# An attention layer's output stage: transposed tiles against numerators scaled in place, eight consecutive tokens per partition

## Chip, core and metric

The kernel runs on one core of a Trainium2 chip, in one launch. Its time is the device time of that core in microseconds. 2926.12 us is the median of three runs before the change (2924.99 to 2928.0). Five engines work side by side, each through its own list of instructions, and meet only at semaphores: TensorE (PE: products, and PEld, its weight loads), VectorE (DVE), ScalarE (ACT), GpSimd (POOL) and SyncE (SP), which here issues nearly all DMAs.

## What is computed

One transformer block with modulation: attention over 16 batches of 1024 tokens with 256 features in 16 heads, then eight experts on rows chosen by index from the first two batches. Cut to what matters here:

```python
h = layernorm(x) * (1 + ca) + sa
xn = layernorm(h) * ln_gamma + ln_beta
q, k, v = heads(xn @ Wq + bq), heads(xn @ Wk + bk), heads(xn @ Wv + bv)   # q, k rotated
probs = softmax(causal(q k^T / 4))
o = (probs @ v) back to (B, L, D)
x = x + ga * (h + o @ Wo + bo)          # the output stage
h2 = layernorm(x) * (1 + cb) + sb       # then the experts, gathered by top_idx
```

`ga` is one row of 256 per batch, so `ga * (o @ Wo)` is `o @ (Wo * ga)`, and `ga * h` is the normalised `x` times a row (`a2`) plus a row that goes with the bias.

## The kernel before

Five stages, each a block with a barrier behind it. phase0 makes constants and the modulation rows. phase1 normalises `x`, projects and rotates it and stores queries, keys and values to HBM in bf16 parts; it also leaves the scale and shift of every row of `x` on chip (`rsx`, `nmx`, row p of tile t being token 128 t + p). phase2 is attention, in 64 units of one batch and four heads. For the unit two ahead TensorE fills PSUM banks with scores, in 19 slots of a unit (L1148, L1155), and VectorE takes their maxima (`largest`, L1069); for the present unit it forms scores again (L1173), ScalarE takes the exponential (L1113), GpSimd cuts the diagonal (L1008) and TensorE weighs the values (L1192). The values carry columns of ones, so that each head's 32 rows of the result are 16 numerators and 16 copies of the sum of the exponentials. `copy_out` (L1101) brings them out of PSUM in two halves, and SP stores them to `att` in HBM (L972).

phase3 is the output stage, batch after batch, in eight tiles of 128 tokens. Per tile TensorE turns four blocks of `att` so that tokens lie in partitions (L1516); VectorE inverts 16 sums (L1420) and multiplies (L1424); TensorE turns the result back (L1524), ScalarE copies it out of PSUM (L1470), and TensorE forms the bias (L1534) and the product with the weights that VectorE scaled by the gate (L1413, L1536). Beside this ScalarE normalises the tile of `x` (L1445), GpSimd multiplies it by `a2` and adds `x` (L1484, L1486, into `res`), and VectorE adds product and `res` (L1432). TensorE's order is written out: the transpositions of tile t, the second turn of tile t - 1, the product of tile t - 2. `res` has room for two batches. SP loads a batch two ahead and stores the finished one (`load`, `load_x`, `store`). In between, spread over batches 2 to 8, the chosen rows of the first two batches are normalised again (`prepare`, `choose`, `scale`): VectorE's statistics in batches 2 and 3, a root on ScalarE in batch 4, then sixteen steps of one instruction on each of three engines. The first experts' weights are loaded in batches 5 to 8, and GpSimd gathers their rows behind batches 12 and 13 (L1257). phase4 runs the experts.

## Time and profile before

| | us |
|---|---|
| median of the runs | 2926.12 |
| the profiled execution | 2926.05 |
| its span, first to last instruction | 2924.3 |
| attention in it (545 to 2338) | 1793 |
| output stage in it (2342 to 2626) | 284 |
| experts in it (2626 to 2916) | 290 |

The span is the time from the first to the last instruction in the trace. A stage is read from its stretch of the trace: how long each engine was busy there, what TensorE's granted clock was (1.00 is 2.4 GHz), and what share of the time the 16 DMA engines moved data. Busy TensorE is not TensorE at its peak, since its instructions overlap; the distance from the start of one to the start of the next tells more.

### The profile page before, as it was taken

The page shows a single profiled execution, that of the slowest core. Times are in us where ns is not written, and L with a number is a line of the kernel's source. Part 1 is how long each engine was busy: PE and PEld are TensorE (multiplying, and loading weights), DVE is VectorE, ACT ScalarE, POOL GpSimd, SP SyncE. Part 2 cuts the span into 40 slices and gives each one's busy share as a digit, 9 for nine tenths or more (in the row PEclk, how much of TensorE's full clock was granted, in tenths as well). Part 3 has the DMA queues.
Part 4 walks back from the last instruction along what each step waited for, and adds up shares of the span by engine and source line. Part 5 has one row for each costly group of instructions (what it writes and reads, how often), then busy time and mean ns, then how long its engine had stood idle before and what let it go on. Part 6 is the DMA issues. An engine that isn't in the chain of part 4 may idle for free. (4 is left out here: it accounts for less than half of the span.)

```text
span 2924.3 us, 48254 instructions
## 1 busy us (share of the span) xinstructions
PE 2748.3 (94%) x17467; PEld 1332.0 (46%) x17467; DVE 2083.7 (71%) x2857; ACT 1823.0 (62%) x3739; POOL 1026.3 (35%) x1554
## 2 busy tenths in 40 slices
PE   3999996999999999999999999999999879989997
PEld 1555552344444444444344443444444256766664
DVE  6999996877777777777777777777777246652221
ACT  2788882477777777777777777777777735432221
POOL 5899973121211212112121111212112158762331
PEclk6999996899999999999999999999999989999999
DMA  4688879345445354453544545444453088952432
GB/s 122 194 261 260 261 236 242 63 84 105 92 93 106 81 109 90 95 101 84 111 88 97 97 89 107 88 101 97 88 107 82 20 284 304 314 196 57 112 92 44
DMA packets 188321, 384.09 MB, mean 131 GB/s; under 512 B 33667, under 2 KB 105795, under 8 KB 175574
## 3 DMA queue, kind: packets, MB, share of 16 engines
q1 hardware_dynamic: 180038, 372.08, 49.9%
q0 software_dynamic: 6144, 8.52, 1.7%
q8 instruction: 141, 2.31, 0.4%
q14 instruction: 94, 0.77, 0.1%
q10 hardware_dynamic: 1904, 0.40, 0.1%
HBM read 238.55 MB, written 144.53 MB: 131 GB/s over the span
## 5 line engine op out<-in xcount | busy, mean ns | idle before, releaser
L1069 DVE TENSOR_REDUCE mx<-ps 128x2 f32<-128x1024 f32 (+3 forms) x1216 | 1371.0, 1166 | 408.6 <-PE ps L1155 313.2
L1113 ACT ACTIVATE prob<-ps 128x512 f32<-128x512 f32 (+1 forms) x2560 | 1251.8, 560 | 526.5 <-PE ps L1173 517.7
L1148 PE MATMUL ps<-k_rows,q_rows 96*128 96x512 bf16 (+3 forms) x3072 | 911.0, 332 | 32.4 <-PEq L420 25.7
L1173 PE MATMUL ps<-q_rows,k_rows 99*128 99x512 bf16 (+3 forms) x3072 | 907.1, 328 | 14.7 <-ACT prob L1113 6.1
L1008 POOL TENSOR_SCALAR_AFFINE_SELECT prob<-prob 128x512 f32<-128x512 f32 x512 | 319.9, 637 | 1451.3 <-ACT prob L1113 1451.3
L1192 PE MATMUL ps<-prob,v_rows 128*32 128x512 f32 (+3 forms) x6144 | 628.3, 496 | 0.0
L1173 PEld LDWEIGHTS ps<-q_rows,k_rows 99*128 99x128 bf16 x3072 | 273.1, 98 | 599.1 <-ACT prob L1113 360.3
L1148 PEld LDWEIGHTS ps<-k_rows,q_rows 96*128 96x128 bf16 x3072 | 290.1, 98 | 262.6 <-DVE mx L1069 60.7
L1155 PE MATMUL ps<-mask_b,unit_b 128*128 128x128 bf16 (+2 forms) x1408 | 348.5, 248 | 0.0
L1192 PEld LDWEIGHTS ps<-prob,v_rows 128*32 128x32 f32 x6144 | 134.3, 108 | 245.8 <-ACT prob L1113 122.9
L792 PE MATMUL ps<-x_t,w_all 128*128 128x512 f32 x512 | 231.6, 595 | 0.0
L1686 DVE SCALAR_TENSOR_TENSOR y<-ps,gx,gate 128x256 f32<-128x256 f32 x32 | 15.5, 484 | 196.4 <-PE ps L1775 196.4
L1155 PEld LDWEIGHTS ps<-mask_b,unit_b 128*128 128x128 bf16 x1408 | 139.4, 99 | 22.9
L1536 PE MATMUL ps<-wg,n_t 128*128 128x256 f32 x512 | 145.7, 407 | 0.0
L747 POOL TENSOR_TENSOR stage<-rest,stage 128x1024 bf16<-128x1024 f32 x64 | 136.7, 2136 | 24.5 <-ACT stage L677 24.5
L1470 ACT COPY n_t<-ps 128x256 f32<-128x256 f32 x128 | 47.5, 371 | 148.6 <-PE ps L1524 148.4
L792 PEld LDWEIGHTS ps<-x_t,w_all 128*128 128x128 f32 x512 | 94.2, 191 | 93.5 <-issue 92.7
L800 PE MATMUL ps<-w_all,x_t 128*128 128x256 f32 x512 | 124.6, 386 | 2.1
L1611 POOL DMA_INDIRECT sum_rows<-ys,dest x32 | 50.1, 1565 | 213.0 <-ACT ys L1698 154.7
L1775 PE MATMUL ps<-w,hid 128*128 128x256 f32 x512 | 119.1, 386 | 0.0
L1484 POOL TENSOR_TENSOR res_b<-res_b,a_b 128x256 f32<-128x256 f32 x128 | 96.3, 753 | 59.1 <-ACT res_b L1445 58.8
L1761 PE MATMUL ps<-gx_t,w 128*128 128x512 f32 x256 | 114.7, 601 | 1.3 <-ACT hid L1706 0.4
(174 smaller groups left out, 2606.4 us busy)
## 6 DMA issues: line engine op xcount, KB each, us to landing
k_rows<-k_parts SPq DMA_DIRECT2D x384, 128.0 KB, 7.3
v_ones<-v_st SPq DMA_DIRECT2D x64, 512.0 KB, 6.5
v_rows<-v_ones SPq DMA_DIRECT2D x64, 512.0 KB, 9.3
att<-o_sb SPq DMA_DIRECT2D x128, 256.0 KB, 2.3
att_b<-att SPq DMA_DIRECT2D x16, 2048.0 KB, 9.9
q_rows<-q_parts SPq DMA_DIRECT2D x64, 384.0 KB, 4.6
q_parts<-stage SPq DMA_DIRECT2D x120, 192.0 KB, 3.3
k_parts<-stage SPq DMA_DIRECT2D x120, 192.0 KB, 3.4
```

Source lines behind the costliest of these rows:

```text
L747: pool.tensor_tensor(parts(n, 2), rest[:, n % 2], parts(n, 1), ALU.subtract).then_inc(lo_done, 1)
L792: ins = pe.matmul(half(n, e), w_all[:, k, c * P:(c + 1) * P], x_t[:, blk, k, :], start=(k == 0), stop=(k == KC - 1))
L800: ins = pe.matmul(o, x_t[:, t // 4, k, t % 4 * P:t % 4 * P + P], w_all[:, k, 2 * D:3 * D], start=(k == 0), stop=(k == KC - 1))
L1008: pool.affine_select(out=own, in_=own, compare_op=ALU.is_ge, fill=0.0, base=0, pattern=[[0, HG], [1, P]], channel_multiplier=-1).then_inc( ...
L1069: dve.tensor_reduce(dst, src, AX.X, ALU.max).then_inc(a_free, 1)
L1113: nc.scalar.activation(prob[:, (g * NPC + i) % RING, h, 0:w], src, ACT.Exp).then_inc(exp_done, 1)
L1148: ins = pe.matmul(ps[:, at, col:col + w], q[g][0:ROWS, h, i * P:(i + 1) * P], k[g][0:ROWS, h, k0:k0 + w], start=(r == 0), stop=True, skip_ ...
L1155: ins = pe.matmul(own, unit_b[:, :], mask_b[:, :].rearrange("p (o n) -> p o n", o=1) .to_broadcast([P, per, P]), start=False, stop=True, s ...
L1173: ins = pe.matmul(ps[:, PS_B + bank(g, n), at:at + w], k[g][0:AUG, h, j * P:(j + 1) * P], q[g][0:AUG, h, q0:q0 + w], start=True, stop=True)
L1192: ins = pe.matmul(ps[32 * h:32 * h + 32, PS_O, col:col + w], v[g][:, j, h, :], prob[:, (g * NPC + i) % RING, h, at:at + w], start=(j == 0) ...
L1536: ins = pe.matmul(o, n_t[:, r % 2, k, :], wg[:, p, k, :], start=False, stop=(k == KC - 1))
L1775: ins = pe.matmul(o, hid[:, f, c * P:(c + 1) * P], w2[:, e % 2, f, :], start=False, stop=(f == FT - 1))
```

## The change

The output stage no longer turns anything. `att` is read as it lies, features in partitions, and only its numerators. The inverses of the sums are made during attention, one batch behind: SP loads a batch's 16 rows of sums into 128 partitions (`load_sums`), VectorE inverts them and splits the result into three bf16 parts (`invert_sums`), SP stores them (`save_inverse`) and later loads them as 48 rows (`load_inverse`). In the output stage TensorE multiplies them with a matrix of ones and zeros (`rows`), which spreads each head's inverse over its 16 features (`spread_rec`, four products of 512 columns per batch), and VectorE multiplies numerators by that (`normalise`, 512 elements each) into `n_t`, from which the product is formed straight away. The four of the next batch stand among the tiles of the present one.

A tile now is every eighth token: partition p holds tokens 8 p to 8 p + 7, so that rows of `x` and of the result are 8 KB of consecutive bytes per partition. `normalise` writes with a step for that, and the scales and shifts of the rows, which phase1 leaves in the other order, go through HBM: SP stores them per batch during attention (`row_stats`) and loads them in the new order. In the last batch of attention SP also loads what the first two or three batches of the output stage need. The product has four PSUM banks in place of two, `x` a ring of three in place of four. In phase0 two pairs of semaphores become one each.

```diff
+def load_sums(sp, o, att_d, b):
+    reuse(sp, o.inv_step, INV_STEPS * b)
+    sums = att_d[b].rearrange("g (h n) t -> (g h) n t", n=2 * (P // HG // 2))[:, P // HG // 2, :]
+    sp.dma_start(o.den[:, :], sums.rearrange("h (a c) -> h a c", c=P)).then_inc(o.den_in, DMA)
...
+def invert_sums(dve, o, b):
+    done = lambda n: INV_STEPS * b + n
+    dve.wait_ge(o.den_in, (b + 1) * DMA)
+    reuse(dve, o.inv_stored, b * DMA)
+    dve.reciprocal(o.inv[:, :], o.den[:, :]).then_inc(o.inv_step, 1)
+    dve.wait_ge(o.inv_step, done(1))
+    dve.tensor_copy(o.inv3[:, 0, :], o.inv[:, :]).then_inc(o.inv_step, 1)
...
+def load_numerators(sp, o, att_d, b):
+    KC = o.num.shape[2]
+    for k in range(KC):
+        mine = att_d[b, k * NG // KC:(k + 1) * NG // KC].rearrange("g (h n) t -> (g h) n t", n=2 * (P // HG // 2))
+        sp.dma_start(o.num[:, b % 2, k, :], mine[:, 0:P // HG // 2, :]).then_inc(o.num_in[b % 2], DMA)
...
                 store(un, 0)
+                output_rows(b, g)
+
+            def output_rows(b, g):
+                if g == 0 and b >= 2:
+                    save_inverse(sp, o, rec_d, b - 2)
+                if g == 1:
+                    with nc.allow_non_contiguous_dma("statistics go to the order of tokens"):
+                        sp.dma_start(stat_d[0, b].rearrange("(t p) -> p t", p=P), rsx[:, b, :]).then_inc(o.stat_stored, DMA)
+                        sp.dma_start(stat_d[1, b].rearrange("(t p) -> p t", p=P), nmx[:, b, :]).then_inc(o.stat_stored, DMA)
...
+                if g == 2 and b >= 1:
+                    for c in range(2):
+                        sp.wait_ge(o_stored[c], b * NG * DMA)
+                    load_sums(sp, o, att_d, b - 1)
+                if g == 2 and b == LAST:
+                    sp.wait_ge(o.stat_stored, 2 * B * DMA)
...
+                    for n in range(2):
+                        load_gate(sp, o, mods_d, out_bias_d, n)
+                        load_numerators(sp, o, att_d, n)
+                        load_inverse(sp, o, rec_d, n)
+                        load_residual(sp, o, x, mods_d, n)
...
+                if g == NG - 1 and b >= 1:
+                    invert_sums(dve, o, b - 1)
...
+            load_sums(sp, o, att_d, B - 1)
             for b in range(B):
+                if b + 2 < B:
+                    load_small(b + 2)
+                    load_num(b + 2)
                 if b + XR - 1 < B and b >= 1:
-                    load_x(sp, b + XR - 1)
+                    load_x(b + XR - 1)
+                if b == 1:
+                    save_inverse(sp, o, rec_d, B - 1)
+                if b + 3 < B:
+                    load_rec(b + 3)
...
+                store(b)
...
+            def normalise(b, q):
+                k, half = q % KC, q // KC
+                at = slice(half * HALF, (half + 1) * HALF)
...
+                dve.wait_ge(spread, b * NQ + q + 1)
+                tiles = lambda v: v.rearrange("d (p t) -> d p t", t=T)
+                dst = n_t[:, b % 2, k, :].rearrange("d (t p) -> d p t", t=T)[:, half * P // 2:(half + 1) * P // 2, :]
+                dve.tensor_tensor(dst, tiles(num[:, b % 2, k, at]), tiles(ps[:, PS_R + q % 2, :]), ALU.mult) \
+                   .then_inc(norm_done, 1)
...
+            for b in range(B):
+                if b + 1 < B:
+                    scale_weights(b + 1)
+                for t in range(T):
+                    if t == 1 and b == 0:
+                        invert_sums(dve, o, B - 1)
+                    finish(b, t)
+                    prepare((b - SB) * T + t)
+                    if t in NORM_AT and b + 1 < B:
+                        normalise(b + 1, NORM_AT.index(t))
...
-                reuse(act, x2_done, b * T - T)
+                reuse(act, x2_done, (b - 2) * T + t + 1)
...
+            for b in range(B):
+                for t in range(T):
+                    product(b, t)
+                    if t in SPREAD_AT and b + 1 < B:
+                        spread_rec(b + 1, SPREAD_AT.index(t))
```

GpSimd's two operations per tile, and its place in the stage, are as they were.

TensorE in the output stage, from the stage's first products on, before the change (`att_b` the transpositions, `norm` the second turn, `ob_b` the bias, `wg` the product):

```order
L1516 MATMUL ps<-ident,att_b 128x128 x8
L1524 MATMUL ps<-ident,norm 128x128 x2
L1516 MATMUL ps<-ident,att_b 128x128 x4
L1524 MATMUL ps<-ident,norm 128x128 x2
L1534 MATMUL ps<-ob_b,ones 128x256
L1536 MATMUL ps<-wg,n_t 128x256 x2
L1516 MATMUL ps<-ident,att_b 128x128 x4
L1524 MATMUL ps<-ident,norm 128x128 x2
L1534 MATMUL ps<-ob_b,ones 128x256
L1536 MATMUL ps<-wg,n_t 128x256 x2
```

The same place in the changed kernel (`head_rows` is the matrix that spreads):

```order
L1641 MATMUL ps<-rec,head_rows 128x512 x4
L1651 MATMUL ps<-ob_b,ones 128x256
L1653 MATMUL ps<-wg,n_t 128x256 x2
L1641 MATMUL ps<-rec,head_rows 128x512
L1651 MATMUL ps<-ob_b,ones 128x256
L1653 MATMUL ps<-wg,n_t 128x256 x2
L1641 MATMUL ps<-rec,head_rows 128x512
L1651 MATMUL ps<-ob_b,ones 128x256
L1653 MATMUL ps<-wg,n_t 128x256 x2
L1651 MATMUL ps<-ob_b,ones 128x256
```

Six transpositions per tile are gone, and four products of 512 columns per batch have come.

VectorE in attention where one unit's maxima end and the next one's begin, behind the last heads of a batch, in the changed kernel (`den` the sums, `inv` their inverse and its parts; before the change the maxima follow one another directly there):

```order
L1190 TENSOR_REDUCE mx<-ps 128x2 x4
L900 RECIPROCAL inv<-den 128x128
L902 CAST inv<-inv 128x128
L904 TENSOR_TENSOR inv_rest<-inv 128x128
L906 CAST inv<-inv_rest 128x128
L908 TENSOR_TENSOR inv<-inv_rest,inv 128x128
L1190 TENSOR_REDUCE mx<-ps 128x2x4
L1190 TENSOR_REDUCE mx<-ps 128x4
```

Five operations of VectorE, with a wait for the load of `den` ahead of them, stand in front of the next unit's first maxima.

SP from the last batch's third unit to the end of attention in the changed kernel, where four stores of `att` stood in a row before:

```order
L1061 DMA att<-o_sb 128x512
L887 DMA den<-att 128x1x128
L1103 DMA rs_wide<-row_stats 128x16x8
L1103 DMA nm_wide<-row_stats 128x16x8
L931 DMA gate_b<-mods 128x256
L932 DMA ob_b<-out_bias_parts 3x256
L920 DMA num<-att 128x1x1024 x2
L913 DMA rec<-rec_sums 48x1024
L926 DMA x_b<-in_L_attn_x 128x2048
L927 DMA a_b<-mods 128x256
```

Behind these come the same loads for the second batch, the rows of a third and its inverses, and only then the last three stores.

## Rows read from the trace of the kernel before

**Rows 1.** Stretches: length, each engine's busy time (instructions), clock, DMA share, GB/s.

```profile
545.00:2338.00 1793.00, 1778.29 (x13562) 727.40 (x13564) 1358.46 (x1360) 1306.70 (x2675) 357.83 (x634) 1.00 0.44 92
2342.00:2626.00 284.00, 254.46 (x1408) 191.32 (x1408) 167.56 (x467) 119.25 (x274) 205.32 (x281) 0.97 0.83 278
```

**Rows 2.** TensorE in order of time, one tile: start, duration, engine, line, operation, operands.

```profile
2444.88 1.13 PE L1536 MATMUL ps<-wg,n_t 128*128 128x256 f32 x4
2445.84 0.60 PE L1516 MATMUL ps<-ident,att_b 128*128 128x128 f32 x4
...
2446.60 0.28 PE L1534 MATMUL ps<-ob_b,ones 3*128 3x256 bf16 x1
2446.80 1.13 PE L1536 MATMUL ps<-wg,n_t 128*128 128x256 f32 x4
```

**Rows 3.** Groups in 2342 to 2626: busy us, mean ns, idle before.

```profile
L1484 POOL TENSOR_TENSOR res_b<-res_b,a_b 128x256 f32<-128x256 f32 x128 | 96.3, 753 | 59.1 <-ACT res_b L1445 58.8
L1486 POOL TENSOR_TENSOR res_b<-res_b,x_b 128x256 f32<-128x256 f32 x128 | 93.5, 731 | 10.0
...
L1424 DVE TENSOR_TENSOR norm<-ps,rec 128x256 f32<-128x256 f32 x128 | 54.3, 424 | 4.6 <-DVE rec L1420 0.2
...
L1432 DVE TENSOR_TENSOR x<-ps,res_b 128x256 f32<-128x256 f32 x112 | 47.5, 424 | 80.0 <-PE ps L1536 77.4 <-POOL res_b L1486 1.6 <-issue 1.1
...
L1420 DVE RECIPROCAL rec<-ps 128x16 f32<-128x16 f32 x128 | 32.1, 251 | 11.5 <-PE ps L1516 10.5
...
L1413 DVE TENSOR_TENSOR wg<-wo,gate_b 128x256 f32<-128x256 f32 x32 | 15.4, 523 | 56.6 <-DMA ob_b<-out_bias_parts 56.6
...
L1257 POOL DMA_INDIRECT gx<-tok_rows,idx x8 | 7.9, 985 | 2.1 <-issue 2.0
...
L1393 DVE BATCH_NORM_STATS2 st<-x_all 128x6 f32<-128x256 f32 x16 | 6.7, 418 | 0.0
```

**Rows 4.** GpSimd in order of time, two tiles near the stage's start.

```profile
2357.04 0.73 POOL L1484 TENSOR_TENSOR res_b<-res_b,a_b 128x256 f32<-128x256 f32 x1
...
2358.53 0.73 POOL L1484 TENSOR_TENSOR res_b<-res_b,a_b 128x256 f32<-128x256 f32 x1
```

**Rows 5.** In order of time: the stage's first transfer, TensorE's first work, last sum.

```profile
2341.70 0.32 SPq L1325 DMA_DIRECT2D gate_b<-mods  x1
...
2350.77 1.97 PE L1516 MATMUL ps<-ident,att_b 128*128 128x128 f32 x8 [12.22 <-DMA att_b<-att]
...
2624.91 0.42 DVE L1432 TENSOR_TENSOR x<-ps,res_b 128x256 f32<-128x256 f32 x1 [0.84 <-PE ps L1536]
```

**Rows 6.** TensorE in order of time, the stage's first product.

```profile
2357.15 2.08 PE L1536 MATMUL ps<-wg,n_t 128*128 128x256 f32 x4
```

**Rows 7.** Attention at a unit's end in order of time: VectorE's maxima, TensorE's fill.

```profile
1408.86 2.36 DVE L1069 TENSOR_REDUCE mx<-ps 128x2 f32<-128x1024 f32 x2 [0.92 <-PE ps L1155]
1412.06 2.36 DVE L1069 TENSOR_REDUCE mx<-ps 128x8 f32<-128x1024 f32 x2 [0.84 <-PE ps L1155]
...
1415.17 0.33 PE L1148 MATMUL ps<-k_rows,q_rows 96*128 96x384 bf16 x1
```

**Rows 8.** VectorE in order of time, in the set-up: a reciprocal, a cast.

```profile
7.90 1.74 DVE L339 RECIPROCAL e<-e 16x256 f32<-16x256 f32 x1
...
39.73 0.23 DVE L626 CAST unit_b<-ident 128x128 bf16<-128x128 f32 x1 [1.84 <-PEq L147]
```

**Rows 9.** SP in order of time: the last batch's third unit is stored.

```profile
2310.95 0.34 SPq L972 DMA_DIRECT2D att<-o_sb  x1
```

**Rows 10.** DMA issues by line: count, size of each, median us to landing.

```profile
tok_rows<-in_L_ffn_combine_weights SPq DMA_DIRECT2D x1, 64.0 KB, 4.6
ident<-in_const_ident SPq DMA_DIRECT2D x1, 64.0 KB, 2.0
```

**Rows 11.** Stretches as in rows 1: the end of attention, a busy batch.

```profile
2290.00:2300.00 10.00, 8.20 (x57) 2.21 (x57) 0.00 (x0) 8.47 (x20) 1.61 (x3) 1.00 0.08 29
2440.00:2457.00 17.00, 15.38 (x88) 11.71 (x88) 11.91 (x31) 8.81 (x20) 14.06 (x20) 1.00 0.95 325
```

307 lines of the change are left out of this document (167 added, 140 removed).

## Prediction

> **What bounds the kernel now.** I read the stages first [rows 1]: attention keeps TensorE busy for 1778 of 1793 us at full clock, and the output stage, which the change rewrites, takes 284 us with TensorE busy for 254, GpSimd for 205 and VectorE for 168. Then the order of one tile on TensorE in the middle of that stage [rows 2]: the product starts at 2444.88, the transpositions of later tiles follow at 2445.84, the bias at 2446.60, the next product at 2446.80. That is 1.92 us per tile without a gap: 0.96 product, 0.76 transpositions, 0.20 bias. Eight tiles are a batch, so TensorE alone needs 15.4 us of the roughly 17 that a batch takes (a sixteenth of the stage below, less its start), and it is the bound. Third, who comes next if TensorE gets less: the groups of that stage [rows 3]. GpSimd does two operations per tile, 753 + 731 = 1484 ns on average; VectorE's are shorter. When nothing holds it back GpSimd starts one tile every 1.49 us, from 2357.04 to 2358.53 [rows 4], so some 12 us per batch. Last the ends of the stage [rows 5]: its first transfer is issued at 2341.70, TensorE begins at 2350.77 after a wait for that data, and the last sum ends at 2624.91 + 0.42 = 2625.33. The stage is 283.6 us long.
>
> The sum goes against the profiled execution, 2926.05 us with a span of 2924.3; the median of the runs shown, 2926.12, is the same within 0.1 us. A difference of 0.2%, about 6 us, is what a measurement of this kernel can tell from none.
>
> **The output stage, TensorE.** The 48 transpositions of a batch go (8 x 0.76 = 6.1 us). Added are four products of 512 columns that spread the inverses; the trace has none here, and the nearest row is the bias, also bf16, 256 columns in 0.20 us [rows 2]. Between 0.2 (if the length cost nothing) and 0.42 each, I take 0.42: 1.7 us. A batch then costs 8 x 1.16 + 1.7 = 11.0 us.
>
> **VectorE.** Eight reciprocals and eight normalisations (251 and 424 ns) go. Four normalisations of 512 elements come, reading PSUM and writing with a step; the row is 424 ns for 256 [rows 3], so 0.42 to 0.85, and up to 1.3 if the step hurts. I take 0.7. With eight sums at 424 and two weight scalings at 523 ns a batch is 2.8 + 3.4 + 1.05 = 7.3 us. Batches 2 and 3 also carry eight statistics of 418 ns each and their small followers, some 12 us in all.
>
> **ScalarE** loses its copies out of PSUM and keeps the row normalisations; it was never late on its own account.
>
> **GpSimd loses nothing**, and so it becomes the bound. Its work is 128 tiles. An operation of 0.73 and its like-sized partner share a pitch of 1.49 [rows 4], so 0.03 us per tile lies between operations; with the averages of [rows 3], which hold the collisions with VectorE's scalings, a tile costs 1.484 + 0.03 = 1.51, together 194 us. Added are 16 multiplications for the chosen rows at about 0.75 (12 us) and the eight gathers (7.9 us and the 2.1 idle ahead of them, 10 us). It starts about 1 us into the stage, since rows, shifts and statistics were loaded during attention, and the last sum takes 0.4. That is 217.2 us against 283.6.
>
> **One stall remains.** In batch 4 ScalarE takes a root for which VectorE must have finished batches 2 and 3. TensorE starts cold: the first products show 2.08 us [rows 6] where the warm row shows 1.13 [rows 2]. Thus VectorE ends batch 3 some 55 us into the stage (5 for the start, about 14, 11, 12.5 and 12.5 for the batches), while GpSimd ends it at 1 + 4 x 12.1 = 49; ScalarE, blocked at the root, feeds it nothing more. I take 5 us, between 0 and 10. Stage: 222.2, so **61.4 us less**.
>
> **Transfers.** A batch now moves 1 MB of numerators (2 MB before), 1 MB of rows in, 1 MB out and 0.35 MB of small things, 3.5 million bytes; in 12.1 us this is 290 GB/s. A busy batch before moved 325 GB/s at a share of 0.95 [rows 11], so they stay just hidden, with a batch of lead. The experts' weights, 1 MB more in batches 5 to 8, fall where GpSimd has 2.9 us more per batch. Over the stage some 58 million bytes; at the stage's own mean of 278 GB/s [rows 1] that is 209 us, below 222.
>
> **Attention.** VectorE gets five operations per batch, between two units. The reciprocal of 128 elements lies between 0.25 us for 16 [rows 3] and 1.74 for 256 [rows 8], linearly 0.95; the four others, 128 elements each, at 0.23 like the cast in [rows 8]. With small gaps 2.0 us (1.6 to 2.8). What hides them: VectorE's last maximum of a unit ends at 1408.86 + 2.36 = 1411.22 and the next starts at 1412.06, 0.84 idle; the second one of that pair ends at 1414.42, and TensorE overwrites its banks at 1415.17, 0.75 later [rows 7]. Less 0.1 for the signal this is a cover of 1.5 us, and 0.5 remains, in which TensorE, the bound there, waits with everything queued behind. Fourteen such places (batch 14's falls where no maxima are left): **7 us more**, between 0 and 18.
>
> SP issues four DMAs more per batch. The two that write the statistics consist of 1024 pieces of 4 bytes each; the nearest row is 64 KB in pieces of 32 bytes, landed after 4.6 us [rows 10]; 2 to 10 us each. Queued behind them are the loads for three units ahead and the maxima of the next unit but one; half a unit, some 14 us, covers them, so I price them at zero. The Trainium skill speaks against them: its page "DMA: Bandwidth & Descriptors" says (Rules for kernel authors) that a non-contiguous last dimension becomes one descriptor per element, and (Specifications) that transfers under 512 B are read, changed and written back. By that they come out dear, and the sum would grow by what exceeds the cover; by the row of 4.6 us it does not change. No run here shows a 4-byte write yet.
>
> At the end of attention SP issues some 6.2 million bytes of first rows and 4096 pieces of statistics behind the store at 2310.95 [rows 9]: 19 us at 325 GB/s plus up to 9, until about 2340; two late stores stand behind them, and the stage began at 2341.70 [rows 5]. **1.5 us more** (0 to 6). In the set-up a wait for the small input now also takes the identity, which lands 2.0 us after its issue [rows 10]: **0.5 us more** (0 to 2).
>
> **Sum:** 2926.05 - 61.4 + 7 + 1.5 + 0.5 = 2873.7, say 2874 us.
>
> **Rivals.** (a) Something else bounds the stage: transfers, or VectorE if the stepped write takes 1.3 us. Transfers decide when the rate falls under 58 / 222 = 261 GB/s; at 240 the stage is 242 us and the time 2893. For it: a batch of lead only and loads that blocked SP before; against it: 325 GB/s in [rows 11]. (b) Nothing of the inversions is hidden: 14 x 2.0 = 28 instead of 7, 2895. For it: TensorE has no gaps in attention; against it: the 0.84 and 0.75 us of [rows 7]. (c) Neither the stall nor the inversions nor the end of attention cost anything: 2926 - 66 = 2860. (d) **Slower than before:** TensorE's clock. GpSimd-bound, TensorE idles for 0.3 us in each 1.5. If the clock then stayed at 1.2 GHz, everything doubles as between [rows 6] and [rows 2], a batch costs 22 us, the stage 352, and the time is about 3003. It decides when the mean batch exceeds 17.1 us, that is when over half of the stage runs slow. Against it stands the end of attention, where TensorE was busy for 8.20 of 10 us, waiting many times for ScalarE, with a granted clock of 1.00 [rows 11]. The Trainium skill has such a case: "TensorE: Matmul & The Clock Gate" (A second HAM failure mode) tells of a kernel whose short pauses between groups of products let the clock swing between its levels; the trace here does not agree, with the 1.00 just named. (e) The 4-byte stores block the queue: slower only if each batch pays over 3.3 us beyond the cover.
>
> **How the numbers follow.** Forecast 0.58, (a) 0.15, (b) 0.10, (c) 0.10, (d) 0.03, (e) 0.02; 0.02 for no change, if TensorE and VectorE keep each other at the old pace. The forecast's own bounds are 2860 to 2890; with (a), (b) and (c) the range is 2858 to 2898. Faster 0.93, same 0.02, slower 0.05.
>
> **What would show it.** Right: the stage some 222 us long, GpSimd busy for about 95% of it, its pitch near 1.5 us, TensorE waiting for VectorE's sums, clock at 1.00 after the start; in attention a gap of about half a microsecond on TensorE behind each batch's reciprocal. Wrong: GpSimd waiting for ScalarE or for rows throughout, TensorE waiting for numerators, a granted clock under 0.9 in mid-stage, or an attention longer by over 20 us.

## The result

The changed kernel takes 2984.61 us (median of 4 runs, 2977.94 to 2990.92) against 2925.97 before (the median of the three runs named above and a fourth): a ratio of 1.020, 95% interval 1.018 to 1.022. It is slower by 59 us where 52 us less were forecast. The profiled execution took 2987.96 us, its span 2986.1, so 61.8 us more than the span before.

The stretches of the changed kernel, attention and output stage (length, busy time and instructions of TensorE, its weight loads, VectorE, ScalarE and GpSimd, granted clock, DMA share, GB/s), stand against [rows 1]:

```profile
545.00:2440.00 1895.00, 1817.55 (x13539) 733.64 (x13537) 1385.12 (x1434) 1310.14 (x2671) 356.20 (x632) 0.97 0.46 91
2445.00:2690.00 245.00, 219.55 (x704) 119.94 (x704) 149.73 (x280) 74.54 (x146) 206.32 (x281) 0.82 0.75 238
```

Attention has grown by some 100 us, and its clock is no longer 1.00. The output stage is shorter, but its clock is 0.82 (before 0.97) and its transfers run at 238 GB/s (before 278). Its ends, in order of time, against [rows 5]:

```profile
2444.87 0.54 SPq L887 DMA_DIRECT2D den<-att  x1
...
2687.14 0.42 DVE L1534 TENSOR_TENSOR x<-ps,res_b 128x256 f32<-128x256 f32 x1 [0.85 <-PE ps L1653]
```

It lasts from 2444.87 to 2687.56, 242.7 us: 40.9 less than before, where 61.4 less were forecast. It begins 103.2 us later than before. Attention proper, from SP's first load of maxima to the output stage's first transfer, takes 1922.3 us in place of 1817.6, so 104.7 more; the set-up in front of it is 1.6 us shorter, the experts behind the stage 0.4.

**The standstills.** Waits by engine, the line that waited and what ended the wait (us in total, times, longest), in attention of the changed kernel:

```profile
ACT prob L1241 <- remote: 57.4, 14, 6.4
DVE mx L1190 <- remote: 52.7, 14, 5.4
...
PEld ps L1276 <- DVE mx L1190: 45.8, 143, 2.5
```

"remote" means that the profile has no event on this core which would explain the end of the wait. There was no such wait before the change. In 15 of the 16 batches such waits end 12 to 19 us after the batch's two stores of `row_stats` were issued; only behind the sixth batch's there is none. One of them, first SP (the two stores of `row_stats`), then ScalarE, VectorE and TensorE, each row with its start and duration:

```profile
2247.54 0.43 SPq L1089 DMA_DIRECT2D row_stats<-rsx  x1
2248.01 1.69 SPq L1090 DMA_DIRECT2D row_stats<-nmx  x1
...
2261.35 2.06 ACT L1241 ACTIVATE prob<-ps 128x512 f32<-128x512 f32 x4 [4.08 <-remote]
...
2261.45 0.96 DVE L1190 TENSOR_REDUCE mx<-ps 128x2 f32<-128x768 f32 x1 [3.11 <-remote]
...
2262.00 0.61 PE L1301 MATMUL ps<-q_rows,k_rows 99*128 99x384 bf16 x2 [2.60 <-ACT prob L1241]
```

The same place in steps of two microseconds, columns as in the stretches above:

```profile
2249.00:2251.00 2.00, 2.00 (x20) 1.24 (x22) 1.27 (x3) 1.72 (x4) 0.03 (x1) 1.00 0.47 16
2251.00:2253.00 2.00, 2.00 (x18) 0.88 (x11) 1.08 (x2) 1.29 (x4) 1.22 (x2) 1.00 0.36 0
2253.00:2255.00 2.00, 2.00 (x18) 0.69 (x16) 2.00 (x2) 0.78 (x3) 0.63 (x1) 1.00 0.00 0
...
2259.00:2261.00 2.00, 0.40 (x4) 0.12 (x2) 0.00 (x0) 0.00 (x0) 0.00 (x0) 1.00 0.00 0
2261.00:2263.00 2.00, 1.00 (x8) 0.43 (x10) 0.96 (x1) 1.65 (x4) 0.00 (x0) 0.59 0.00 0
2263.00:2265.00 2.00, 2.00 (x14) 0.90 (x14) 1.30 (x3) 1.30 (x4) 1.22 (x2) 0.50 0.00 0
```

The small pieces occupy the DMA engines until about 2253 and move next to nothing (the share is 0.36 at 0 GB/s). Some six microseconds later all four engines stand still at once, and ScalarE and VectorE go on within 0.1 us of each other. TensorE then works at half clock (0.50) for a while. A batch thus loses the standstill, and TensorE's work behind it at the lower clock comes on top; how the loss divides between the two is not measured.

**The end of attention.** ScalarE, and SP, whose three last stores of `att` are folded into one row with the time from the first to the last:

```profile
2441.65 0.58 ACT L1229 COPY o_sb<-ps 128x512 f32<-128x512 f32 x1 [11.13 <-DMA att<-o_sb]
```

```profile
2422.53 20.09 SPq L1061 DMA_DIRECT2D att<-o_sb  x3
```

The last copy out of PSUM waited 11.13 us for a store that stood behind the preloads.

**In the output stage**, groups of instructions (busy us, mean ns, idle before and what ended it), against [rows 3]:

```profile
L1609 POOL TENSOR_TENSOR res_b<-res_b,a_b 128x256 f32<-128x256 f32 x128 | 97.5, 762 | 22.0 <-ACT res_b L1579 21.7 <-issue 0.3
L1611 POOL TENSOR_TENSOR res_b<-res_b,x_b 128x256 f32<-128x256 f32 x128 | 94.3, 736 | 10.0
L1579 ACT ACTIVATE res_b<-x_b,nm_wide,rs_wide 128x256 f32<-128x256 f32 x128 | 66.6, 588 | 142.7 <-DMA a_b<-mods 131.1 <-DVE x_all L1534 9.0 <-PEq L987 2.7
L1524 DVE TENSOR_TENSOR n_t<-num,ps 128x512 f32<-128x512 f32 x64 | 66.1, 1039 | 19.5 <-DMA num<-att 16.9 <-PE ps L1653 2.4
...
L1511 DVE TENSOR_TENSOR wg<-wo,gate_b 128x256 f32<-128x256 f32 x32 | 23.3, 768 | 39.3 <-PEq L987 34.9 <-DMA ob_b<-out_bias_parts 4.4
```

GpSimd's operations are nearly as long as before (762 and 736 ns, 753 and 731 before), and it is busy for 206 of 243 us, that is 85%, not 95%. ScalarE, which feeds it, waited 131 us for rows. The normalisation takes 1.04 us, not 0.7.

### The profile page after: what moved, and what is told of

Read it like the earlier page. It is cut to its first block and busy times, and to the rows that moved or that the text cites. A ratio compares the mean times of both kernels' runs of the same rounds, so it can differ in the third digit from the quotient of the medians.

```text
span 2986.1 us, 46292 instructions
## 1 busy us (share of the span) xinstructions
PE 2753.6 (92%) x16763; PEld 1268.2 (42%) x16763; DVE 2092.3 (70%) x2746; ACT 1783.4 (60%) x3611; POOL 1022.4 (34%) x1554
## 2 busy tenths in 40 slices
DMA packets 202793, 371.66 MB, mean 124 GB/s; under 512 B 78099, under 2 KB 119507, under 8 KB 185958
## 5 line engine op out<-in xcount | busy, mean ns | idle before, releaser
L1301 PE MATMUL ps<-q_rows,k_rows 99*128 99x512 bf16 (+3 forms) x3072 | 920.3, 333 | 59.1 <-ACT prob L1241 48.8
L1320 PE MATMUL ps<-prob,v_rows 128*32 128x512 f32 (+3 forms) x6144 | 641.9, 506 | 0.0
L1653 PE MATMUL ps<-wg,n_t 128*128 128x256 f32 x512 | 173.0, 468 | 0.0
L1579 ACT ACTIVATE res_b<-x_b,nm_wide,rs_wide 128x256 f32<-128x256 f32 x128 | 66.6, 588 | 142.7 <-DMA a_b<-mods 131.1
L1653 PEld LDWEIGHTS ps<-wg,n_t 128*128 128x128 f32 x512 | 102.1, 221 | 29.2 <-issue 6.9
```

The costliest lines, as they stand in the source:

```text
L1301: ins = pe.matmul(ps[:, PS_B + bank(g, n), at:at + w], k[g][0:AUG, h, j * P:(j + 1) * P], q[g][0:AUG, h, q0:q0 + w], start=True, stop=True)
L1320: ins = pe.matmul(ps[32 * h:32 * h + 32, PS_O, col:col + w], v[g][:, j, h, :], prob[:, (g * NPC + i) % RING, h, at:at + w], start=(j == 0) ...
L1653: ins = pe.matmul(c, n_t[:, b % 2, k, t * P:(t + 1) * P], wg[:, b % 2, k, :], start=False, stop=(k == KC - 1))
```

## The experiments

All times stand against the kernel before, measured on the same chip in the same series (medians 2925.97 to 2928.06). The sections up to the inversions are about attention. Lengths of a stage come from the one profiled execution of each kernel; the runs of one kernel of the later sections lie up to 22 us apart, so a few microseconds between two such stages tell little.

### Is it the 4-byte stores? The change without them

```diff
-                if g == 1:
-                    ... sp.dma_start(stat_d[0, b].rearrange("(t p) -> p t", p=P), rsx[:, b, :])
-                    ... sp.dma_start(stat_d[1, b].rearrange("(t p) -> p t", p=P), nmx[:, b, :])
+                if g == 1 and b == 0:
+                    sp.wait_ge(o.stat_copied, 1)
+                    sp.dma_start(stat_d.rearrange("n b (t p) -> (b t) n p", p=P), o.stat[:, :, :])
...
+                for n, src in enumerate((rsx, nmx)):          # TensorE, ahead of attention
+                    ins = pe.transpose(ps[:, PS_O, n * P:(n + 1) * P], src..., ident[:, :])
```

> The changed kernel, with one thing different: the 32 stores of row_stats in pieces of 4 bytes are gone. TensorE turns rsx and nmx once, ahead of attention (two transpositions into the bank of the results), ScalarE copies them out, and SP stores them with one DMA of 256 pieces of 512 bytes. Theory A (the 4-byte stores make all engines stand still for 2 to 6 us, 11 to 15 us after their issue, and cool TensorE's clock): the waits named remote vanish, the output stage begins near 2354 instead of 2445, the time falls by about 90 us to 2890 to 2900, below the kernel before. Theory B (the inversions or the DMAs that belong to them cause the standstills, 15 of them too): the output stage still begins near 2440 and the time stays near 2980. Theory C (the time in attention goes into both): in between, and the rest then shows at the inversions on VectorE.

Measured: 2898.95 us (4 runs), ratio 0.990, interval 0.988 to 0.992. The output stage begins at 2355.03, and no wait is named remote. So 85.7 us of the changed kernel's time hang on these 32 stores, 5.4 per batch, and without them the change is a gain. Theory A.

### The stores alone, on the kernel before

```diff
                 store(un, 0)
+                if g == 1:
+                    for n, src in enumerate((rsx, nmx)):
+                        sp.dma_start(stat_d[n, b].rearrange("(t p) -> p t", p=P), src[:, b, :])
```

> The kernel before, and nothing of the change in it but the 32 stores of row_stats in pieces of 4 bytes (two per batch, behind the store of the second unit's first half), which nobody reads. Theory A (these stores alone stop the engines): one standstill per batch 11 to 15 us behind them, attention longer by 80 to 95 us, the time 3005 to 3020. Theory B (the inversions cause it): within 10 us of 2926.

Measured: 3036.12 us in one run, 110 more than before: 6.9 us per batch. One standstill, in steps of two microseconds (the stores were issued at 940.59 and 941.07):

```profile
950.00:952.00 2.00, 1.58 (x20) 0.89 (x12) 0.52 (x2) 0.00 (x0) 0.20 (x1) 1.00 0.00 0
952.00:954.00 2.00, 0.00 (x0) 0.00 (x0) 0.00 (x0) 0.00 (x0) 0.00 (x0) 1.00 0.00 0
954.00:956.00 2.00, 0.00 (x0) 0.00 (x0) 0.00 (x0) 0.00 (x0) 0.00 (x0) 0.80 0.00 0
956.00:958.00 2.00, 0.83 (x4) 0.39 (x4) 0.96 (x1) 1.09 (x2) 0.00 (x0) 0.50 0.00 0
```

ScalarE and VectorE, as they go on:

```profile
956.51 1.09 ACT L1120 ACTIVATE prob<-ps 128x512 f32<-128x512 f32 x2 [7.07 <-remote]
956.66 0.96 DVE L1076 TENSOR_REDUCE mx<-ps 128x2 f32<-128x768 f32 x1 [6.14 <-remote]
```

TensorE's last products before this ended near 951.6, and both engines wait here only for semaphores that TensorE's products raise, so what they waited for was done 5 us earlier. The stores stop the engines with nothing else of the change present. The loss was even larger than expected (3005 to 3020).

### The same bytes in pieces of 32 bytes

```diff
-sp.dma_start(stat_d[n, b].rearrange("(t p) -> p t", p=P), src[:, b, :])
+sp.dma_start(stat_d[n, b].rearrange("(p t) -> p t", p=P), src[:, b, :])
```

> The kernel before with the same 32 stores of the same bytes at the same places, but in pieces of 32 bytes (each partition's eight values stay together; nobody reads them). If the number of pieces decides (128 instead of 1024 per store): no standstill, within 5 us of 2926. If two more stores per batch on SP's queue decide, whatever their pieces: as with the 4-byte stores, 3005 to 3020. If an HBM write below 512 bytes decides by itself: standstills shorter in the ratio of the pieces, 0.6 us each, 2935.

Measured: 2926.49 us, one run: no cost, no standstill. Two more stores per batch on SP's queue are harmless by themselves.

### 4-byte loads in place of stores

```diff
-sp.dma_start(stat_d[n, b].rearrange("(t p) -> p t", p=P), src[:, b, :])
+sp.dma_start(spare[:, n, b, :], x_flat[b, n * L:(n + 1) * L].rearrange("(t p) -> p t", p=P))
```

> The kernel before with 32 loads in pieces of 4 bytes (1024 pieces each, 4 KB of x into a spare tile, at the places where the stores of row_stats would be; nobody uses them). If 4-byte pieces stop the engines in either direction, by their number: standstills and 3010 to 3036, as with the stores. If only small writes to HBM do: no standstill, within 5 us of 2926; a few us more at most from queueing on SP.

Measured: 2927.55 us, one run: no cost. The number of pieces and their size do not do it in the direction of reading.

### Half as many stores

```diff
-for n, src in enumerate((rsx, nmx)):
+for n, src in enumerate((rsx,)):
```

> The kernel before with only one of the two 4-byte stores per batch (rsx, 1024 pieces; nobody reads them). Both together cost 110 us, 6.9 per batch. If the standstill is proportional to the pieces: 2975 to 2985. If a fixed time per batch or per event: 3020 to 3036. If only what exceeds some room that hides the first pieces counts: 2930 to 2960.

Measured: 2930.4 us, one run, 4 more than before, and inside the range of the kernel before in the same series (2923.46 to 2931.13); attention is 2.6 us longer, and no wait is named remote. Half the pieces do not cost half. There is room in which they cost nearly nothing, and beyond it the cost is steep.

### 4-byte stores 512 bytes and 64 bytes apart

```diff
-stat_d = nc.dram_tensor("row_stats", [2, B, L], F32, ...)
+stat_d = nc.dram_tensor("row_stats", [2, B, L, P], F32, ...)     # second kernel: 16 in place of P
...
+sp.dma_start(stat_d[n, b, :, 0].rearrange("(t p) -> p t", p=P), src[:, b, :])
```

> The kernel before with both 4-byte stores per batch, each piece 512 bytes from the next one in HBM (the receiving tensor has 128 places per value, one is written; nobody reads them). If the standstill comes from neighbouring pieces falling into the same line of memory from several DMA engines at once: gone or small, 2926 to 2945. If every small write costs by itself: as when they lie side by side, 3010 to 3040.

> The kernel before with both 4-byte stores per batch, each piece 64 bytes from the next one (512 bytes apart they cost nothing, side by side 110 us; nobody reads them). If the pieces disturb each other only within 64 bytes: 2922 to 2930. If the unit in which they collide is larger, up to 512 bytes: in the ratio of neighbours, 8 instead of 128 in 512 bytes, 2930 to 2945, or as side by side, 3036.

Measured: 2923.75 us with 512 bytes between them, 2928.67 with 64, one run each: no cost in either. The same 32768 small writes are free when they lie 64 bytes apart. So it is not the small write by itself that costs, but many small writes beside each other.

### The two stores half a batch apart

```diff
-                if g == 1: rsx and nmx
+                if g in (1, 3): rsx at 1, nmx at 3
```

> The kernel before with both 4-byte stores per batch side by side in HBM, but half a batch apart: rsx behind the second unit's first half, nmx behind the fourth's. One store alone per batch cost 4 us in all, both together 110. If the time that the standstill takes grows once the pieces outstanding together exceed what is hidden: 2930 to 2936, twice the 4 us. If the number of pieces per batch decides, or nmx's place in memory: 3010 to 3036.

Measured: 2933.05 us, one run: 7 more than before in place of 110, and of that only 1.0 us in attention (1818.6 us in place of 1817.6). As many neighbouring small writes, but fewer of them at once, stop nothing.

### The same in the changed kernel

```diff
                     sp.dma_start(stat_d[0, b]..., rsx[:, b, :])
-                    sp.dma_start(stat_d[1, b]..., nmx[:, b, :])
+                if g == (3 if b < LAST else 0):
+                    sp.dma_start(stat_d[1, b]..., nmx[:, b, :])
```

> The changed kernel with one line moved: nmx is stored half a batch after rsx (behind the fourth unit's first half, in the last batch behind the first's), still in pieces of 4 bytes side by side. Theory A (what stops the engines is the number of neighbouring small writes under way at once; on the kernel before this spacing took the cost from 110 to 7 us): no long standstills, the output stage begins near 2357, 2899 to 2910, much as with the turned statistics. Rival (in the changed kernel the further DMAs of the inversions lie close enough to bring the standstill back): 2940 to 2985.

Measured: 2904.2 us (2 runs), ratio 0.992, interval 0.990 to 0.995. The output stage begins at 2353.55. No wait is named remote. One moved line turns the loss of 59 us into a gain of 22.

### The inversions alone

```diff
+                if g == 0 and b >= 2:
+                    save_inverse(sp, o, rec_d, b - 2)
+                if g == 2 and b >= 1:
+                    for c in range(2):
+                        sp.wait_ge(o_stored[c], b * NG * DMA)
+                    load_sums(sp, o, att_d, b - 1)
...
+                if g == NG - 1 and b >= 1:
+                    invert_sums(dve, o, b - 1)
```

> The kernel before with only the inversions added in attention: SP loads a batch's sums, VectorE inverts and splits them between two units, SP stores the three parts, which nobody reads; the output stage is as before. By the prediction's term (0.5 us uncovered at each of 14 places): plus 7 us, 2933, with a range of 0 to 18. By its rival (nothing is hidden): plus 28, 2954. If the inversions were what stops the engines: 3005 to 3020.

Measured: 2932.2 us (9 runs), ratio 1.0021, interval 1.0011 to 1.0031, so 3 to 9 us more; attention itself grows by 6.7. VectorE's groups in it:

```profile
L878 DVE RECIPROCAL inv<-den 128x128 f32<-128x128 f32 x15 | 14.1, 943 | 25.8 <-DMA den<-att 25.8
L886 DVE TENSOR_TENSOR inv<-inv_rest,inv 128x128 bf16<-128x128 f32 x15 | 4.9, 324 | 0.5
```

With the other three (292, 227 and 226 ns) a batch's five operations take 2.0 us. The one wait of 25.8 us lies at attention's end, where VectorE has no maxima left. What VectorE waited for TensorE's scores, and TensorE's weight loads for VectorE's maxima, before and with the inversions:

```profile
DVE mx L1069 <- PE ps L1155: 286.0, 370, 0.9
PEld ps L1148 <- DVE mx L1069: 32.2, 123, 0.3
```

```profile
DVE mx L1121 <- PE ps L1210: 264.7, 341, 0.9
PEld ps L1203 <- DVE mx L1121: 41.0, 151, 0.4
```

Of the 30 us of new work some 21 went into VectorE's own idle time, and TensorE waited 8.8 us more. The forecast's 7 us stands, and most of the work is hidden, as it said; the cover of 1.5 us per place was not measured by itself.

### The end of attention: late stores ahead of the preloads

From here on each kernel is held against the one with turned statistics (2899). All but the old order of tokens, which needs no statistics in HBM, contain its repair.

```diff
-                    for n in range(2): gate, numerators, inverses, rows     # all behind the third unit
-                    load_residual(sp, o, x, mods_d, 2)
+                    first_rows(0)                                           # behind the third unit
+                if g == 3 and b == LAST:
+                    first_rows(1)                                           # no rows of x
...
             def epilogue():
                 store(unit(LAST, NG - 1), 1)
+                load_residual(..., 1); load_residual(..., 2)
```

> The kernel with turned statistics (2899), and the preloads at the end of attention spread out: behind the third unit of the last batch only what batch 0 needs, behind the first store of the last unit the small things and numerators of batch 1, and the rows of batches 1 and 2 behind the very last store of att. Theory A (the late store waits behind 6 MB of preloads: ScalarE waits 8.9 us for it, and the block's end waits for SP, whose three late issues hold 18 us): the output stage begins 8 to 10 us earlier, near 2345; rows of batches 1 and 2 come later, at most 3 us given back; 2890 to 2893. Rival (what was moved is only paid later, in the stage, which is bound by transfers): within 3 us of 2899.

Measured: 2888.63 us (4 runs), ratio 0.987, interval 0.984 to 0.990; the stage begins at 2350.42 and lasts 243.5 us. ScalarE's last copy out of PSUM waits 1.87 us in place of 8.88. Of the 8.9 us between the two spans 4.1 are attention's and 4.3 the stage's (247.8 without this edit). That is near Theory A's time (2890 to 2893), but the stage begins 4.6 us earlier and not 8 to 10. The medians lie 10 us apart and the four runs of each kernel 12 and 17 us, so the size of the gain is uncertain. This kernel has the lowest median of the study among those that compute everything; four later ones (2889.3 to 2897.05) lie within its range of 2883.08 to 2899.8. It is faster than both given kernels.

### The old order of tokens

```diff
-x[b].rearrange("(p t) d -> p t d", p=P)
+x[b].rearrange("(t p) d -> p t d", p=P)
...
-                dve.tensor_tensor(dst, tiles(num...), tiles(ps...), ALU.mult)      # dst with a step
+                dve.tensor_tensor(n_t[:, b % 2, k, at], num[:, b % 2, k, at], ps[:, PS_R + q % 2, :], ALU.mult)
```

> The changed kernel with the old order of tokens: a tile is 128 consecutive tokens again, the rows of x and of the result move in pieces of 1 KB, the multiplication by the inverses writes without a step, and rsx and nmx are used as phase1 leaves them, so that no statistics go through HBM at all (no 4-byte stores, no loads of 32-byte pieces). Inverses, numerators, preloads, rings and orders stay as in the change. Theory A1 (the new order of tokens gains nothing but the stepped write costs): the multiplication falls from 1.04 to about 0.6 us, the time lies 5 to 15 us below the 2899 of the kernel with turned statistics, 2885 to 2894. Theory A2 (pieces of 8 KB are what makes transfers fast): the stage gets longer by about 10 us, 2905 to 2912. Theory A3 (neither matters, the order in which SP issues the loads bounds the stage): 2895 to 2902.

Measured: 2909.52 us (4 runs), ratio 0.994, interval 0.993 to 0.996, and a stage of 255.3 us. The multiplication falls to 677 ns as expected, and still the stage is 7.5 us longer than with turned statistics: as Theory A2 had it, pieces of 8 KB are worth more than the step costs. That VectorE's shorter work brought nothing also speaks against VectorE as the bound of the stage.

### TensorE kept warm at the start, and the root later

```diff
+            for n in range(8):                       # behind the last product of attention
+                keep_warm(pe, ps[:, 1, :], ident)
...
                 spread_rec(0, q)
+                for n in range((0, 2, 1, 2)[q]):
+                    keep_warm(pe, ps[:, 6, :], ident)
...
-    FIRST_H = NT + 6                                 # second kernel only
+    ROOT = NT + 10
+    FIRST_H = ROOT + 4
```

> The kernel with turned statistics and late stores first (2889), and thirteen products of TensorE whose result nobody reads: eight behind the last product of attention, where it waits about 7 us for the end of the stage, and five between the four that spread the first batch's inverses, where it waits for VectorE. Theory A (TensorE starts the stage at half clock because it stood still, and batch 0 takes 24 us instead of 13): the granted clock stays at 1.00 through the start, batch 0 ends some 10 us earlier, 2876 to 2882. Rival 1 (GpSimd's 208 us bound the stage anyway; the lost start is caught up): within 3 us of 2889. Rival 2 (the clock falls all the same at the waits for VectorE): within 3 us of 2889, the clock at 0.50 until 2376.

> As the next kernel (later rows behind the late stores, TensorE kept warm), and ScalarE's root for the chosen rows with all that hangs on it one batch later (eight tiles). Theory A (the root blocks ScalarE, because VectorE has not finished batches 2 and 3; 7.9 us at it, and GpSimd starves for some 20 us around 2385 to 2430): a further 5 to 10 us less than the next kernel, 2866 to 2876, with GpSimd busy for over 9 of 10 us from 2360 on. Rival (VectorE and the transfers are what is late there, the root only shows it): within 2 us of the next kernel.

Measured: 2894.64 us (0.988, 0.987 to 0.990) warm, 2889.3 (0.987, 0.985 to 0.988) warm and with the later root, against 2888.63 for the kernel both are built on: no gain that can be told (the runs of the three overlap). Ten microseconds behind the stage's start, without the warm products:

```profile
2360.00:2370.00 10.00, 10.00 (x22) 4.97 (x22) 6.35 (x10) 2.40 (x4) 9.53 (x14) 0.50 0.30 75
```

and with them:

```profile
2360.00:2370.00 10.00, 8.99 (x36) 4.98 (x34) 8.73 (x15) 3.67 (x7) 9.45 (x14) 1.00 0.30 90
```

The clock is 1.00 in place of 0.50 and TensorE does 36 instead of 22 products, yet the stage is 243.5 us long in both. What the start gains is waited for later: the cold start costs nothing as long as something else is late. Rival 1 of that expectation said this, but named GpSimd as the bound, which the last experiment does not bear out for this kernel; and 2894.64 lies outside its 3 us. With the later root the stage was 249.8 us long, in the slowest of that kernel's four runs (2899.72); the gain of 5 to 10 us that was expected of it did not come.

### Deeper rings, all repairs together, and gates early

```diff
-                    load_num(b + 2)                  # two buffers, waits for the fifth tile
-                    load_x(b + 2)                    # three buffers, queued behind it
+                    load_x(b + 3)                    # four buffers
+                    load_num(b + 3)                  # three buffers
...
-                    load_small(b + 2)                # third kernel only: gates in a ring of four
+                    load_small(b + 3)
```

> The kernel with turned statistics (2899), and deeper rings in the output stage: three buffers of numerators in place of two, four of rows in place of three (the added ones lie where queries and keys of the first unit lay), and SP issues both for the batch three ahead at the head of a batch, where nothing that they wait for is still open; the kernel before it issued numerators of two ahead behind the fifth tile, and rows behind these. Theory A (late issue makes ScalarE wait 133 us for rows and VectorE 21 us for numerators, and TensorE's clock falls in these waits): waits fall below 30 us, the stage from 248 to 222 to 230 us, 2873 to 2882. Rival (the transfers' rate is the bound, 58 MB at 270 GB/s): the waits stay, the stage is 240 or more, 2890 to 2899.

> All four repairs at once: turned statistics, late stores ahead of preloads, deeper rings with loads three batches ahead, TensorE kept warm and the root one batch later. If each was held back by the others (rings by the root, which grew to 25 us there; the warm start by rows that are late): 2868 to 2880. If the transfers' rate bounds the stage whatever the order: 2885 to 2895, as each alone.

> All four repairs together, and the gates' rows (which the weights are scaled by) in a ring of four, loaded three batches ahead like the rest; with all repairs but this one VectorE waited 51 us for the gate and the bias, which queue behind megabytes of rows and numerators issued before them. Theory A (small loads that land late are what took the gain of the deeper rings): that wait vanishes, the stage falls from 255 to 226 to 235 us, 2870 to 2882. Theory B (what moves in the stage, at the rate that the 16 engines reach, bounds it, and each order only shifts who waits): the wait moves to rows, numerators or inverses, 2885 to 2900.

Measured: 2897.05 us (0.990, 0.988 to 0.991) with rings alone, 2900.45 (0.989, 0.986 to 0.992) with all four repairs, 2891.23 (0.989, 0.987 to 0.991) with the gates too. The stage lasts 251.2, 255.5 and 239.1 us. With rings alone ScalarE's waits for rows fell from 133 to 66 us, but VectorE now waited 46 us for the gate's row, and ScalarE 25 at the root. All four repairs together came out above both expectations; their runs spread from 2882.39 to 2904.52, and the profile is of the slowest. There VectorE waits for the gate and the bias, and ScalarE still 65 us for rows:

```profile
DVE wg L1542 <- DMA ob_b<-out_bias_parts: 51.3, 12, 7.3
```

With the gates early VectorE's wait is gone, and these are the longest (with those for the fourth buffer of rows, 25.7, ScalarE's come to 85):

```profile
ACT res_b L1610 <- DMA a_b<-mods: 59.6, 7, 11.5
DVE x L1566 <- DMA out<-x: 40.8, 11, 9.8
```

Whatever is issued first, something else is late: first the rows, then the gates, then the stores of finished results, whose buffers are not free. This is what Theory B of the last expectation said, and 2891.23 lies in its range.

### Fewer transfers

```diff
-                if b + XR - 1 < B and b >= 1:
-                    load_x(b + XR - 1)
...
```

> The kernel with turned statistics and late stores first (2889), with the rows of x loaded for the first three batches only; what is left out: batches 3 to 15 add the rows of an earlier batch instead of their own, so that 14.8 MB of some 58 fewer are moved in the output stage. Theory A (the rate of the transfers, some 265 to 280 GB/s, bounds the stage): the stage falls from 245 to about 212, GpSimd's 208 us and its start, the time to 2855 to 2865. Theory B (the order of SP's issues, the cold start or the root bound it): within 8 us of 2889.

The kernel leaves out the rows of `x` of batches 3 to 15 and adds those of an earlier batch in their place, so its result is not the block's. By the trace's totals it moves 15.3 MB less (371.66 and 356.31), not 14.8.

Measured: 2875.57 us (2 runs), ratio 0.983, interval 0.981 to 0.985, against 2888.63 for the kernel it is built on. The stage lasts 225.7 us in place of 243.5. Its longest waits now are

```profile
ACT res_b L1588 <- DVE x L1543: 79.0, 68, 6.2
DVE x L1543 <- POOL res_b L1620: 45.5, 39, 5.6
```

ScalarE waits for room, VectorE for GpSimd, which is busy for 206 of 226 us: only now is GpSimd the bound, as the prediction had it for the changed kernel. So 13 us (between the medians) to 18 (between the profiled stages) hang on these loads. That is less than the 24 to 34 of Theory A and more than the 8 of Theory B. The edit also takes 26 DMAs out of SP's queue, so it does not part the rate of the transfers from their order.

## Why the prediction was wrong

**The step that failed first: the stores of `row_stats`, priced at zero.** The prediction saw 1024 pieces of 4 bytes, took 2 to 10 us each from [rows 10] and covered them with the half unit of SP's queue behind them. It priced the wrong resource. The loads behind the stores were hardly late (in attention keys landed 7.7 us after their issue on the median, 7.2 before the change; maxima 9.5, 9.1 before). Instead all engines stood still, the last of it 12 to 19 us after the issue, and TensorE's clock fell to 0.50 in both standstills shown. 85.7 us hang on it in the changed kernel, 110 on the kernel before. Rival (e) put the point at 3.3 us per batch and got 5.4, but as a blocked queue and with a chance of 0.02; it had no row for a 4-byte write and should have kept a wide end in the range. The rule of the Trainium skill that was weighed there ("DMA: Bandwidth & Descriptors", Rules for kernel authors and Specifications: one descriptor per element, writes under 512 B read, changed and written back) spoke in the right direction. The runs agree only in part: the same small writes 64 bytes apart cost nothing, so neither the descriptors nor the single small write are the price.

**The output stage, forecast 222.2, measured 242.7.** The step that failed is "they stay just hidden". The mean of 278 GB/s in [rows 1] was taken for what the stage can move at any time, and 58 million bytes came out as 209 us. But it moves little at its ends. The kernel before, its first 30 us:

```profile
2345.00:2375.00 30.00, 21.10 (x104) 16.05 (x104) 11.38 (x33) 8.82 (x21) 15.63 (x22) 0.74 0.91 308
```

The kernel with late stores first, its first 30 us, its middle and its last 30:

```profile
2345.00:2375.00 30.00, 22.56 (x59) 10.80 (x52) 16.03 (x24) 12.66 (x24) 22.88 (x33) 0.60 0.47 140
2375.00:2570.00 195.00, 174.09 (x597) 96.66 (x595) 125.37 (x238) 58.60 (x115) 165.69 (x225) 0.90 0.86 278
2570.00:2600.00 30.00, 21.82 (x68) 12.40 (x69) 11.00 (x27) 4.05 (x8) 17.45 (x25) 0.77 0.25 101
```

Where transfers ran at 308 GB/s at the start of the stage, they now run at 140, because SP waits there to store batch 0 before it may load more: it issues nothing from 2356.70 to 2376.39. In the changed kernel SP issues nothing from 2451.23 to 2465.97, when the store of batch 0 goes out, and its first 24 us are

```profile
2445.00:2457.00 12.00, 9.61 (x20) 4.37 (x21) 10.35 (x16) 9.00 (x18) 11.01 (x16) 0.50 0.36 99
2457.00:2469.00 12.00, 12.00 (x43) 6.54 (x42) 7.61 (x15) 3.60 (x6) 11.37 (x17) 0.90 0.24 91
```

The middle then has to carry the rest. With 15.3 MB fewer the stage takes 225.7 us, within 3.5 of the forecast, and there GpSimd is the bound. In the changed kernel itself it is not, so the mechanism of the forecast failed along with the number: the term of the transfers was zero in place of 13 to 18, measured on the kernel with late stores first. Rival (a) named transfers, with a stage of 242 us at 240 GB/s; the trace has 242.7 us and 238 GB/s. That these agree proves nothing more, since the mean rate is the same 58 million bytes over the length of the stage, whatever makes it long; what speaks for (a) are ScalarE's 131 us of waiting for rows and the kernel with fewer of them. Three signs of being wrong that the prediction named were there: ScalarE waiting for rows, a clock under 0.9, and attention longer by over 20 us.

**Smaller terms.** The inversions: 7 us forecast, 5.9 measured, right. The end of attention: 1.5 forecast; the wait was 11.13 us, and spreading the preloads brought back some 10 between the medians, about half of it in the stage. The step behind it took the last transfer at 2340 and the stage's old begin for a cover, and forgot that a copy out of PSUM waits for the store behind the preloads, and that the block's end waits for SP; it also counted two late stores where three stood behind the preloads. The set-up: 0.5 forecast, it got 1.6 shorter. The root's stall: 5 forecast; ScalarE waited 9.8 for it, and moving it gained nothing that can be told. The normalisation: 0.7 taken, 1.04 measured, inside its bounds of 0.42 to 1.3 and without effect, since VectorE is busy for 150 of 243 us.

**Rival (d), the clock.** The rows of the changed stage show it swing between its levels (0.50 and 1.00, 0.82 on the mean), so what the prediction quoted against it, 1.00 at the end of attention in [rows 11], did not carry over. The Trainium skill's case of a clock that swings with short pauses ("TensorE: Matmul & The Clock Gate", A second HAM failure mode) thus agrees with the trace as far as the swinging goes. At the start it was not what cost time: with 1.00 in place of 0.50 there, the stage was as long. For the middle no run tells. There are stretches such as this one of the changed kernel, in which TensorE is busy throughout at 0.50 and GpSimd for 3.38 of 12 us:

```profile
2505.00:2517.00 12.00, 12.00 (x26) 6.33 (x26) 5.63 (x16) 3.56 (x6) 3.38 (x6) 0.50 0.69 220
```

SP's loads stand behind stores of sums that wait for TensorE's products, so a slow TensorE can make rows late, and late rows can slow TensorE; which came first is not shown, and a part of the 20 us over the forecast may be the clock's. The stage as a whole was not doubled, as (d) had it.

Added up against the profiled execution: attention takes 1832.2 us in the kernel with turned statistics and 1922.3 in the changed one, so 90.2 for the stores; 6.7 for the inversions, measured alone; what is left of the 104.7, 7.9, for the end of attention. With 40.9 less in the stage and 2.0 less at both ends of the program this gives 61.8, the difference of the spans. It closes by construction, since the 7.9 is a remainder. The stage was 5.1 us longer with turned statistics than in the changed kernel, so the 85.7 between the medians is net of that.

**What stays open.** Why neighbouring small writes stop engines that have nothing to do with them is not shown: the trace tells only that ScalarE and VectorE got a signal some 5 us after the work it stands for. Nor is it shown whether the stage is held by the rate of the 16 engines, by the order in which their queue is served, or in part by TensorE's clock. Against the rate alone speaks that their share in the middle was 0.83 to 0.89 in every variant that loads all rows, at 254 to 278 GB/s, while the kernel before had

```profile
2375.00:2570.00 195.00, 182.42 (x1026) 137.32 (x1024) 125.16 (x353) 89.61 (x205) 148.23 (x203) 1.00 0.92 307
```

But no order of issue that was tried brought the stage under 239.1 us.

## What to carry to other kernels

A DMA that writes words of 4 bytes side by side, many at a time, can cost far more than its bytes, and not on its queue: look for waits that no event on the core ends, and turn the data on chip before it leaves, or spread the stores in time. To space the words 64 bytes apart also took the cost away, on the kernel before. Where an operation of a kind that the trace has never shown enters a loop, keep its dear end in the range, even when its queue seems to have cover. And a mean rate over a stage is no proof that transfers are hidden; count what can move while the first batch is still at work.

## What the runs showed of the hardware

- On the kernel before, 1024 writes of 4 bytes side by side per batch cost at most 4 us in all sixteen batches (2930.4, one run), 2048 at once 110 us (3036.12), and the same 2048 at a distance of 64 or 512 bytes nothing (2928.67 and 2923.75 us against 2926). Loads of 4 bytes cost nothing (2927.55).
- In the two standstills shown TensorE, VectorE, ScalarE and GpSimd all stop, after the DMA engines have already fallen idle (share 0.00). The longest such wait was 6.4 us in the changed kernel and 7.7 with the stores alone.
- In the kernel with turned statistics TensorE began the output stage at a granted clock of 0.50, worked without a gap from 2359.80 on and was at 1.00 from 2380 on; with products kept up across the end of attention it was at 1.00 throughout the start.
- VectorE's product of 512 elements from PSUM takes 677 ns with a plain write and 1039 with a stepped one.
